# Moving DVE's result work and the row transposes between the blocks of a mixture-of-experts kernel, and splitting the first product of the prologue

## The reference, cut to what matters

```python
score = softmax(xf @ Wg + bg); gate = max(score); idx = argmax(score)      # 8192 x 16
# each expert takes its first 512 rows; later ones get zero
h = relu(einsum('ecd,edh->ech', buf, W1) + b1)                             # 512 -> 2048
y = einsum('ech,ehd->ecd', h, W2) + b2                                     # 2048 -> 512
x = x + gb * where(keep, y[idx, pos] * gate, 0)
```

## Time and profile before

| | |
|---|---|
| median of 3 runs | 1816.24 us (1816.03 to 1816.32) |
| profiled execution | 1814.79 us |
| its span, first to last instruction | 1813.2 us |
| granted clock of TensorE, mean | 0.995 |
| TensorE, matmul records | 1779.8 us busy (98%) |
| DVE / ACT / POOL | 61% / 49% / 34% |
| chain that ended last | PE 89% |

### The profile page before, as it was taken

One profiled execution on the slowest core, in us unless ns is written; L12 is line 12 of the kernel. 1 busy time (PEld: TensorE's weight loads), 2 busy tenths in 40 slices (PEclk: granted clock), 3 DMA queues, 4 the chain that ended last, 5 costly groups with the idle time before them and its releaser, 6 DMA issues.

```text
span 1813.2 us, 27903 instructions
## 1 busy us (share of the span) xinstructions
PE 1779.8 (98%) x9135; PEld 1489.6 (82%) x9136; DVE 1112.3 (61%) x1964; ACT 893.4 (49%) x1317; POOL 610.1 (34%) x565
## 2 busy tenths in 40 slices
PE   9999999999999799999999999998998999999998
PEld 5788888888888488898888888888888888888886
DVE  6577887887887644445445444457558675444753
ACT  4446546546546344354444444347467664434741
POOL 1145555555554511123030303043225431304303
PEclk9999999999999899999999999999999999999999
DMA  7586767777777454344453524265446553426522
GB/s 278 183 228 186 197 157 204 180 173 200 188 193 221 95 174 160 112 168 167 144 169 107 174 98 162 98 207 197 158 141 225 197 212 129 155 98 211 201 80 79
DMA packets 148429, 304.09 MB, mean 168 GB/s; under 512 B 18097, under 2 KB 18493, under 8 KB 146326
## 3 DMA queue, kind: packets, MB, share of 16 engines
q1 hardware_dynamic: 115098, 221.01, 35.0%
q0 software_dynamic: 33280, 82.42, 18.8%
HBM read 254.29 MB, written 67.43 MB: 177 GB/s over the span
## 4 chain that ended last, share of the span: by engine, by line
PE 89%; DVE 1%; ACT 1%; issue 1%; DMA 1%; POOL 0%; POOLq 0%; ACTq 0%; DVEq 0%
PE bank L344 27%; PE bank L346 27%; PE bank L345 27%; PE bank L778 3%; PE bank L962 1%; PE bank L875 1%; PE bank L649 1%; PE bank L770 1%; DMA h_rows<-xr 1%; ACT h_f L1304 0%; PE bank L753 0%; ACT h_hi L1303 0%; PE bank L748 0%; DVE w_lo L1746 0%; PE bank L785 0%
## 5 line engine op out<-in xcount | busy, mean ns | idle before, releaser
L1303 ACT ACTIVATE h_hi<-bank,b_col 128x512 fp32r<-128x512 f32 x256 | 176.8, 691 | 526.1 <-PE bank L346 474.9
L1773 DVE TENSOR_TENSOR h_lo<-h_f,h_hi 128x512 fp32r<-128x512 f32 x256 | 174.0, 691 | 349.9 <-ACT h_f L1304 270.7
L344 PE MATMUL bank<-bt_hi,w_hi 128*128 128x512 f32 (+4 forms) x1024 | 359.1, 351 | 3.9 <-DVE w_lo L1746 3.5
L345 PE MATMUL bank<-bt_lo,w_hi 128*128 128x512 f32 (+4 forms) x1024 | 358.0, 350 | 0.0
L346 PE MATMUL bank<-bt_hi,w_lo 128*128 128x512 f32 (+4 forms) x1024 | 358.0, 350 | 0.0
L344 PE MATMUL bank<-w_hi,h_hi 128*128 128x512 f32 x832 | 325.8, 392 | 1.0 <-issue 1.0
L345 PE MATMUL bank<-w_lo,h_hi 128*128 128x512 f32 x832 | 324.2, 390 | 0.0
L346 PE MATMUL bank<-w_hi,h_lo 128*128 128x512 f32 x832 | 323.9, 389 | 0.0
L2069 POOL DMA_INDIRECT out_dram<-yo,tok_x x64 | 75.4, 1178 | 671.7 <-DVE yo L1808 636.4
L344 PEld LDWEIGHTS bank<-bt_hi,w_hi 128*128 128x128 f32 x1024 | 193.2, 189 | 28.8 <-issue 5.6
L345 PEld LDWEIGHTS bank<-bt_lo,w_hi 128*128 128x128 f32 x1024 | 193.3, 189 | 21.2 <-issue 0.2
(11 more groups left out here) (312 smaller groups left out, 2938.0 us busy)
## 6 DMA issues: line engine op xcount, KB each, us to landing
raw<-in_L_ffn_W_dram SPq DMA_DIRECT2D x128, 1024.0 KB
xa<-in_L_attn_x_dram SPq DMA_DIRECT2D x16, 1024.0 KB, 8.5
xr<-in_L_attn_x_dram SPq DMA_DIRECT2D x16, 1024.0 KB, 6.8
xr<-global_rows POOLq DMA_DIRECT2D x16, 1024.0 KB, 8.6
h_rows<-sb_tab SPq DMA_DIRECT2D x16, 1024.0 KB
out_dram<-xr SPq DMA_DIRECT2D x16, 1024.0 KB, 10.7
h_rows<-h POOLq DMA_DIRECT2D x15, 1024.0 KB
b_bc<-in_L_ffn_b_dram SPq DMA_DIRECT2D x16, 256.0 KB, 6.3
```

What stands on the lines that cost most here:

```text
L344: pe.matmul(o, a_hi, b_hi, start=start, stop=False)
L345: pe.matmul(o, a_hi, b_lo, start=False, stop=False)
L1303: act.activation(h1_hi[b % 2][:, j, :], h_bank[j][:, :], ACT.Relu, bias=bias)
L1773: dve.tensor_tensor(h1_lo[b % 2][:, j, :], h1_f[:, j, :], h1_hi[b % 2][:, j, :].bitcast(F32), ALU.subtract) \
```

## The change

Four edits among the experts: `gate_results` goes from the end of block 1 to block 0, right behind `result_rows`; `add_results` goes from the end of block 2 to behind `w1_low` of that block; `rows_low` goes ahead of `w2_low` of block 3; and `between`, with the next expert's transposes, goes from ahead of tile 0 into its middle, behind six of its twelve matmuls. In the prologue M is formed in three rounded matmuls per pair of chunks instead of one unrounded: ACT makes the high halves of wk and wq, DVE the low halves, into space that m and v take later, so that the split of M waits for all four copies; two more warm-up matmuls stand ahead.

```diff
+    wk_hi, wk_lo = over(r_v, ("wk_hi", full, F32R), ("wk_lo", full, F32R))
+    wq_hi, wq_lo = over(r_m, ("wq_hi", full, F32R), ("wq_lo", full, F32R))
...
-        for _ in range(6):
+        for _ in range(8):
             pe.matmul(banks[7][:, 0:P], ident[:], ident[:], start=True, stop=True)
         for k in range(KC):
-            pe.wait_ge(wqk_in[k], 32)
+            pe.wait_ge(pro_hi_done, 2 * k + 2)
             for c in range(KC):
-                last = pe.matmul(pro_bank(MCH + c)[:, :], wq_s[:, k, chunk(c)], wk_s[:, k, :],
-                                 start=(k == 0), stop=(k == KC - 1))
+                pe.matmul(pro_bank(MCH + c)[:, :], wq_hi[:, k, chunk(c)], wk_hi[:, k, :], start=(k == 0), stop=False)
+            pe.wait_ge(split_made, 2 * k + 2)
+            for c in range(KC):
+                pe.matmul(pro_bank(MCH + c)[:, :], wq_hi[:, k, chunk(c)], wk_lo[:, k, :], start=False, stop=False)
+                last = pe.matmul(pro_bank(MCH + c)[:, :], wq_lo[:, k, chunk(c)], wk_hi[:, k, :], start=False,
+                                 stop=(k == KC - 1))
...
-            between()
             tile(0)
...
             def tile(j):
                 for c in range(HC):
+                    if between is not None and j == 0 and c == HC // 2:
+                        between()
                     last = split3(pe, y_bank[j][:, :], h1_hi[b % 2][:, c, chunk(j)], h1_lo[b % 2][:, c, chunk(j)],
...
+        for k in range(KC):
+            act.wait_ge(wqk_in[k], 32)
+            act.activation(wk_hi[:, k, :], wk_s[:, k, :], ACT.Copy).then_inc(pro_hi_done, 1)
+            act.activation(wq_hi[:, k, :], wq_s[:, k, :], ACT.Copy).then_inc(pro_hi_done, 1)
         act.wait_ge(cond_in, 16)
...
+        for k in range(KC):
+            dve.wait_ge(pro_hi_done, 2 * k + 1)
+            dve.tensor_tensor(wk_lo[:, k, :], wk_s[:, k, :], wk_hi[:, k, :].bitcast(F32), ALU.subtract) \
+                .then_inc(split_made, 1)
+            dve.wait_ge(pro_hi_done, 2 * k + 2)
+            dve.tensor_tensor(wq_lo[:, k, :], wq_s[:, k, :], wq_hi[:, k, :].bitcast(F32), ALU.subtract) \
+                .then_inc(split_made, 1)
+
         dve.wait_ge(sc_step, 1)
...
+        dve.wait_ge(pro_evac, MCH + KC)
         split_weights(MCH, [t[:] for t in m_f], m_hi, m_lo, 0)
...
                     w1_low(n + 1, (b + 1) % 2)
+                if b == 2 and not first:
+                    add_results(e - 1)
                 for j in range(1, HC):
                     split_hidden(e, b, j)
+                if b == NB - 1 and not last:
+                    rows_low(e + 1)
                 w2_low(n, b)
...
                 if b == 0 and not first:
                     result_rows(e - 1)
-                if b == 1 and not first:
                     gate_results(e - 1)
                 if b == 2:
                     if not first:
-                        add_results(e - 1)
                         dve.wait_ge(y_ready, 4 * e)
...
-            if not last:
-                rows_low(e + 1)
```

More of the change, by code:

```diff
@@ L264, in build_block @@
     sc_step = sem("sc_step")
-    cast_made, split_made, wv_hi_done, hg_step = (sem(k) for k in ("cast_made", "split_made", "wv_hi_done", "hg_step"))
+    cast_made, split_made, pro_hi_done, hg_step = (sem(k) for k in ("cast_made", "split_made", "pro_hi_done", "hg_step"))
     fix_step, mod_fixed = sem("fix_step"), sem("mod_fixed")
@@ L366, in build_block @@
     FIRST_TAB = 11
-    SPLIT_WV, SPLIT_M, SPLIT_WO, SPLIT_V = 0, KC, 2 * KC, 3 * KC
+    SPLIT_WV, SPLIT_M, SPLIT_WO, SPLIT_V = 2 * KC, 3 * KC, 4 * KC, 5 * KC
     DVE_MADE = 7
@@ L939, in rows_of, with filled_tiles @@
             return pe.value_load(expert_rows[0:1, bass.ds(e, 1)], min_val=0, max_val=T)
-        def filled_tiles(rows, tile, passed_over=lambda: None, between=lambda: None):
+        def filled_tiles(rows, tile, passed_over=lambda: None):
             for j in range(GS - 1, 0, -1):
@@ L998, in hidden, with results @@
             narrowest(range(256, ROWS + 1, 64))
-        def results(e, b, rows, between=lambda: None):
+        def results(e, b, rows, between=None):
             n = NB * e + b
@@ L1020, in passed_over @@
                     pe.sem_inc(y_full, 1)
-            filled_tiles(rows, tile, passed_over, between)
+            filled_tiles(rows, tile, passed_over)
         def first_expert():
@@ L1076, in _ @@
         for k in range(KC):
-            act.activation(wv_hi[:, k, :], wv_s[:, k, :], ACT.Copy).then_inc(wv_hi_done, 1)
+            act.activation(wv_hi[:, k, :], wv_s[:, k, :], ACT.Copy).then_inc(pro_hi_done, 1)
         for c in range(KC):
@@ L1396, in _ @@
         for k in range(KC):
-            dve.wait_ge(wv_hi_done, k + 1)
+            dve.wait_ge(pro_hi_done, 2 * KC + k + 1)
             dve.tensor_tensor(wv_lo[:, k, :], wv_s[:, k, :], wv_hi[:, k, :].bitcast(F32), ALU.subtract) \
                 .then_inc(split_made, 1)
+        dve.wait_ge(pro_evac, MCH + KC)
         split_weights(MCH, [t[:] for t in m_f], m_hi, m_lo, 0)
```

## The result

| | before | changed |
|---|---|---|
| median of 6 runs each, us | 1816.28 (1815.85 to 1817.07) | 1824.62 (1822.76 to 1826.91) |
| ratio, 95% interval | | 1.0045 (1.0032 to 1.0058) |
| profiled execution, us | 1814.79 | 1822.76 |

The change made the kernel 8.3 us slower. The direction was forecast (+3.85 us), the size was not: 1824.62 lies above the range's end of 1822.7.

The account below looks back on a forecast made before the run. TensorE, busy 98% of the span, was taken as the bound. Handovers, one-tile experts and prologue gave 6.45 - 2.6 + 0 = +3.85 us on the 1816.24 median: 1820.0 us, bounds 1817.5 to 1822.7, stated range 1813.5 to 1822.7.

Parts of the forecast that it names:

- Low halves of the rows ahead of w2's low half: In the experts: w2's split and two 1 MB loads come later, but well before first use; claimed to cost nothing.
- Handovers: Between experts: with transposes mid-tile, 2.67 us of cover against a 3.08 us sequencer chain; 6.45 us lost on 13 handovers.
- rival A: At handovers: the sequencer gets further ahead than 17 matmuls, so the chain stays hidden; 1814.8 us, chance 0.13.
- One-tile experts: In two experts: w1 wait goes, relu's end stays, six matmuls fewer before the hidden matmul; 1.3 us won each, 2.6 together.
- rival B: In the one-tile experts: the next w1 lands earlier, so the relu waits go too; 1810.2 us, chance 0.10.
- Prologue: Score matrix product ends 2.2 us earlier, but TensorE then idles for the second wmod block; gain 0.
- rival C: In the prologue: the wmod block lands earlier and the 2.2 us get through, L597 at 19.6; 1817.8 us, chance 0.08.
- Additions, gating: In the expert blocks: additions ahead of splits of hidden rows, and gating in block 0, each claimed to change nothing.
- Rival D: A handover costs 1 us, with a late weight load and a clock fall in the prologue; 1825 us, chance 0.07.

Follow-up runs that it names:

- experiment 1: Changed kernel, rows' low halves back behind w2's low half in expert 0: +4.4 us against before; kernel before, new order its only edit: +3.7 us.

## Why the prediction fell short

- **Low halves of the rows ahead of w2's low half: "nothing".** This step failed. I saw that w2's split moves by 11 us and two loads of 1 MB behind it, and asked only when their data are used. I did not ask what else moves by DMA at their new time. TensorE's first entry into the expert loop does; +3.9 us (experiment 1), as much as the whole forecast. Of these 2.3 us are the longer idle time and 1.6 us the half clock behind it. The 0.99 us put down to "issue" ahead of the first results was in the trace of before, and I had no row for it.
- **Handovers: +6.45.** Mechanism right (17 matmuls in hand, a chain of 3 us), rival A wrong; measured 5.6. Four into 512 columns at 0.5 came to 0.55 to 0.59. The Trainium skill (Advanced Engine Details and Errata, Engine Queue Depths) gives TensorE's queue a depth of 64; at two entries for a weight load and its matmul, an estimate, that would have hidden the chain. The trace shows 17 pairs once more, and the measurement decides. Over-sized were the first, into 448 columns (0.6 against 0.11), two into 256 columns behind eight transposes (0.45 against 0.30 and 0.32), and the two behind experts of two tiles (0.25 against 0.08 and 0.09).
- **One-tile experts: -2.6.** The wait for w1 went, relu did not move, rival B did not come true: right. Measured 0.0 and -1.4, and the 1.4 is luck. The term counted six matmuls fewer behind relu and left out two things: the wait for bt_lo behind them, 1.06 us in the second expert, and the clock. In the 5.53 us from which I took the 1.4 the clock stood at half, for which I had no row. It fell in the first expert in the changed kernel and in the second in the kernel before, so that the first lost by it what it had won and the second got back what it had cost.
- **Prologue: 0.** The 0 came out by luck, and the step behind it, that the 2.2 us end at wm_b, was wrong. It rested on one landing of that load, 13.9 us after its issue. In the changed kernel's trace it landed after 11.8 us, the first small product started at 19.68, the sign that I had given for rival C, and 1.8 us got through to expert 0's transposes, where the late fourth gather took them. In the six other traces with the new prologue TensorE stood idle for the load, as forecast, for 1.1 to 2.6 us. Not in the sum either: that the prologue costs elsewhere. Alone it measured +2.85, perhaps in part through the program's length.
- **Additions, gating**: the additions were not run alone; gating measured +1.4, with an interval that holds no change, where I had "nothing" outside the one-tile experts, and it is in those that the trace shows it.
- **Range and rivals.** The bounds that I gave for handovers and one-tile experts add up to 1816.4 to 1823.7, not to 1817.5 to 1822.7; the measured time lies above both. Rival D names 1825, but not the cause: no handover cost 1 us, and the clock stayed at 1.00 in the prologue.

## What to carry to other kernels

When an edit moves a wait, list the DMAs behind it on their queue and look for whoever else needs the DMA engines at the new time, the fetching of code at a first pass included. Before moving work out from behind a chain of control, count what the sequencer has in hand when the chain begins. A wait removed ahead of another wait only changes sides: first find what ends the last one (here a load, which issued earlier turned a loss into a gain). A term that rests on when one load landed in one execution needs the landing of other executions beside it.

## What the runs showed of the hardware

- At the first pass through the expert loop one branch of TensorE's sequencer took 4.0 to 4.7 us in the eleven traces without two loads of 1 MB issued 2 to 4 us ahead of it, 5.9 to 6.6 us in the five with them. In the kernel before the same branch runs 45 times, 0.17 us at the median.
- A load of one count into a register, with what belongs to it, held TensorE's sequencer 0.76 us (1576.61 to 1577.36 in the changed kernel).
- Half clock followed idle stretches irregularly: a wait of 3.20 us in the changed kernel was followed by a granted clock of 0.50, one of 3.59 us in the same trace by 1.00; and 2.9 us was followed by 0.50 to 0.58 in the three kernels that lengthen the program, two by unread increments and one by the new prologue alone, 2.98 us in the kernel before by 1.00.
- The same load of 1 MB in the prologue landed 11.8 to 14.2 us after its issue, and the slowest of four gathers of 128 rows 3.5 to 5.5 us after its own, in sixteen traces.
